# A decoder layer with routed experts: eight expert tiles are run between the last routing steps

## What is computed

```python
logits = xf @ Wg.T
topw, topi = jax.lax.top_k(jax.nn.softmax(logits), 2)
topw = topw / topw.sum(axis=-1, keepdims=True)
for e in range(16):
    h = silu(xf @ W1[e]) * (xf @ W3[e])
    out = out + gates[:, e:e + 1] * (h @ W2[e])
```

## Time and profile before

| what | us |
|---|---|
| median of 3 runs | 822.67 (821.59 to 822.88) |
| the profiled execution | 823.12 |
| its span, first to last instruction | 821.3 |
| PE busy in the span | 798.6 (97%) |
| POOL busy in the span | 396.8 (48%) |
| mean granted clock of PE | 0.993 |

### The profile page before, as it was taken

How to read it: one execution, slowest core, us unless ns; L and a number is a source line. 1 busy time by engine, 2 the same in 40 slices (tenths; PEclk the granted TensorE clock), 3 DMA queues, 4 the chain that set the end, 5 groups by cost and what they waited for, 6 DMA issues and landing times.

```text
span 821.3 us, 21021 instructions
## 1 busy us (share of the span) xinstructions
PE 798.6 (97%) x5949; PEld 758.3 (92%) x5950; DVE 598.0 (73%) x1722; ACT 432.8 (53%) x1185; POOL 396.8 (48%) x567
## 2 busy tenths in 40 slices
PE   9999999999999999999999999999988999999995
PEld 8898999999999999999999999999987799999994
DVE  4757777888787877878787778887675566666663
ACT  4473554637265463737355453726243267667673
POOL 3332134444534454454535444353435358787875
PEclk9999999999999999999999999999999999999997
DMA  8786573655739284564828375573499458777780
GB/s 266 256 290 233 194 256 120 244 204 193 256 125 308 81 281 161 201 242 160 280 95 309 108 254 175 187 263 127 156 425 368 146 106 134 127 132 128 131 132 2
DMA packets 105673, 161.19 MB, mean 196 GB/s; under 512 B 10672, under 2 KB 69616, under 8 KB 104752
## 3 DMA queue, kind: packets, MB, share of 16 engines
q1 hardware_dynamic: 79264, 115.33, 42.0%
q0 software_dynamic: 15792, 35.17, 17.2%
q10 hardware_dynamic: 10576, 10.19, 4.7%
HBM read 50.14 MB, written 112.47 MB: 198 GB/s over the span
## 4 chain that ended last, share of the span: by engine, by line
PE 82%; DVE 6%; ACT 6%; issue 3%; DMA 1%; SPq 1%; POOL 1%; POOLq 0%; DVEq 0%; ACTq 0%
PE ps L797 70%; PE ps L808 5%; PE ps L1037 3%; PE ps L1147 2%; PE ps L1169 2%; ACT fT_hi L1305 2%; ACT relu_v L1306 2%; ACT phi L1292 1%; DVE fT_lo L1508 1%; DVE snmax L1681 1%; DVE smax L1677 1%; DVE pr L1670 1%; DVE xn_attn L1501 0%; ACT pr L1351 0%; DVE stat L1490 0%
## 5 line engine op out<-in xcount | busy, mean ns | idle before, releaser
L788 POOL DMA_INDIRECT out<-narrow,sidx x79 | 122.4, 1549 | 46.1 <-DVE sidx L1886 20.7
L1220 ACT ACTIVATE xn3T<-ps 128x512 f32<-128x512 f32 x17 | 10.2, 597 | 138.8 <-PE ps L808 136.2
L797 PE MATMUL ps<-w_hi,fT_hi 128*128 128x256 f32 x256 | 79.8, 312 | 2.4 <-DVE fT_lo L1508 2.1
L1292 ACT ACTIVATE phi<-ps,nmax 128x128 f32<-128x128 f32 x256 | 73.4, 381 | 9.2 <-DVE nmax L1629 9.0
L1508 DVE TENSOR_TENSOR fT_lo<-relu_v,fT_hi 128x512 fp32r<-128x512 f32 x64 | 52.3, 818 | 33.2 <-ACT relu_v L1306 33.0
L797 PE MATMUL ps<-w_lo,fT_hi 128*128 128x256 f32 x256 | 72.3, 282 | 0.0
L797 PE MATMUL ps<-w_hi,fT_lo 128*128 128x256 f32 x256 | 72.2, 282 | 0.0
L1306 ACT ACTIVATE relu_v<-ps,b_sb 128x256 f32<-128x256 f32 x128 | 69.1, 540 | 0.0
L1305 ACT ACTIVATE fT_hi<-ps,b_sb 128x256 fp32r<-128x256 f32 x128 | 68.0, 531 | 1.5 <-PE ps L797 1.5
L605 POOL TENSOR_TENSOR veps<-mv,eps_ln 128x2 f32<-128x2 f32 x48 | 10.8, 225 | 118.4 <-DVE mv L1494 118.4
L797 PE MATMUL ps<-hT_hi,w_hi 128*128 128x256 f32 x256 | 67.2, 284 | 0.0
(11 more groups left out here) (300 smaller groups left out, 2744.6 us busy)
## 6 DMA issues: line engine op xcount, KB each, us to landing
expert_rows<-zero_rows SPq DMA_DIRECT2D x16, 4352.0 KB, 16.0
narrow<-expert_rows ACTq DMA_DIRECT2D x71, 136.0 KB
expert_up_hi<-X SPq DMA_DIRECT2D x16, 352.0 KB, 2.7
e_lo<-expert_up_lo POOLq DMA_DIRECT2D x2, 2816.0 KB, 12.8
e_hi<-expert_up_hi POOLq DMA_DIRECT2D x2, 2816.0 KB, 22.1
part_raw<-in_E SPq DMA_DIRECT2D x30, 176.0 KB
expert_up_lo<-part_raw SPq DMA_DIRECT2D x15, 352.0 KB, 3.1
X<-in_x SPq DMA_DIRECT2D x16, 256.0 KB
```

Of the source, the lines that this page charges most:

```text
L788: pool.indirect_dma_start(out_rows, bass.IndirectOffsetOnAxis(sidx[:, u:u + 1], 0), yg[:, u, :], None, bounds_check=NT * P - 1, oob_is_err ...
L797: return pe.matmul(out_, lhsT, rhs, start=start, stop=stop)
L1220: return act.activation(out_, in_, ACT.Copy)
L1292: last = act.activation(phi[:, g, h, :], ps[:, g, h * M:(h + 1) * M], ACT.Exp, bias=nmax[:, g, h:h + 1])
```

## The change

Eight slots become early ones. Their plan is made in turns 16 and 17 from the counts of the first 13 sequences (`early_count`, `early_order`, `early_tiles`, `early_taken`, `early_waits` on DVE): experts are ordered by their number of full tiles, and the first eight full tiles in that order are slots 0 to 7. By the counts above these are seven of expert 14 and one of expert 7. SP loads them in turn 17 (`load_early`). Turn 18 goes away: the router of the last sequence, its choice, its counts, its place and its stores are written between slots 0 and 1 of the experts, the plan of the other 71 slots between slots 1 and 3.

The text of the last router on PE now stands ahead of slot 0 (`last_router_rows`, `router(NSEQ - 1, 4)`); ACT copies the rows of the last sequence (`own_rows`) behind the first two roundings; POOL computes the odds with a power (`choice_odds`), which ACT did with an exponential before, and gathers the edges between scatters 1 and 2 (`gather_edges`). The meeting of tiles is worked out in slots 9 to 11, now from both ends of the two tiles, and SP holds slot 8 for it. For the early slots a slot of another expert always counts as meeting, and slots 8 and 9 always wait for slots 6 and 7.

`yg` and `sidx` become rings of 16 (`RING`); `xg` stays at 8. ACT loads tiles 8 to 13 at one place, at the end of slot 6 (`load_late`). The weights are loaded earlier: the low up parts of 14 experts in turn 15, and all up parts by SP. 24 slots are written out, then three rounds of 16, then 7. The matmuls that only kept PE busy behind the last cross attention and ahead of the experts (`keep_clock`: 8, then 9 and 10 calls, and 2 ahead of the last count) go away.

```diff
+    EARLY = 8
+    RING = 2 * GB
+    EARLY_SEQS = NSEQ - 3
+    UNROLLED = 3 * GB
 ...
-            for u in range(GB):
-                step(u, u, False)
-            with eng.Fori(0, (SLOT_TILES // GB - 2) // 2) as g:
+            for s in range(UNROLLED):
+                step(s, s % RING, False)
+            with eng.Fori(0, (SURE - UNROLLED) // RING) as g:
 ...
                 if last_cross:
+                    load_early()
 ...
+            def load_early():
+                sp.wait_ge(early_plan, EARLY_TILES)
+                sp.wait_ge(zeroed, 16 * (NSEQ + 1))
+                sp.wait_ge(placed, EARLY_SEQS * 16 * TOPK * TS)
+                tiles = [tile_of(s) for s in range(3)]
+                sp.wait_ge(snmax_ready, NSEQ)
+                for s in range(GB):
+                    load_tile(s, tiles[s] if s < len(tiles) else tile_of(s))
 ...
-                if isinstance(s, int) and s == 1:
+                if isinstance(s, int) and s == EARLY:
                     sp.wait_ge(ranges_ready, 1)
 ...
+            choice_odds()
+            store_rows(NSEQ - 1)
+            in_groups(slot_tiles, pool)
 ...
-                if last_cross:
-                    keep_clock(2, 7)
-                if b is not None and not last_ffn:
+                if b is not None and not last_ffn and not last_cross:
                     turn_router_rows(b, 7)
 ...
-            keep_clock(2, 10)
+            last_router_rows()
             turn_rows(0, 0)
             turn_rows(1, 1)
+            router(NSEQ - 1, 4)
+            pe.wait_ge(em_loaded, 16 * 6)
             up(0, 0)
 ...
+                if first(s):
+                    count_choices(NSEQ - 1, 5)
+                    pe.wait_ge(logit_ready, NSEQ)
+                if isinstance(s, int) and s == 1:
+                    pe.wait_ge(ps_read, 2)
+                if isinstance(s, int) and s == 3:
+                    pe.wait_ge(plan_ready, 1)
 ...
+            def load_late():
+                act.wait_ge(plan_ready, 1)
+                tiles = [tile_of(s) for s in range(EARLY, EARLY + 2)]
+                act.wait_ge(placed, NSEQ * 16 * TOPK * TS)
+                for s in range(EARLY, 2 * EARLY - 2):
+                    load_rows(s, s, tiles[s - EARLY] if s - EARLY < len(tiles) else tile_of(s))
 ...
+                if isinstance(s, int) and s == EARLY - 2:
+                    load_late()
+                    rows_hi(s + 2, (u + 2) % RING)
 ...
+                if first(s):
+                    place_own(NSEQ - 1, 5)
+                    dve.wait_ge(egap_ready, NSEQ)
+                    gates(NSEQ - 1)
 ...
+                if isinstance(s, int) and s == 1:
+                    late_count()
+                    late_sum()
+                if isinstance(s, int) and s == 2:
+                    late_tiles()
 ...
-                if isinstance(s, int) and s in (1, 2, 3):
-                    (edge_rows, meeting_tiles, numbers_of_tiles)[s - 1]()
+                if isinstance(s, int) and s == EARLY + 1:
+                    edge_rows()
+                if isinstance(s, int) and s == EARLY + 2:
+                    meeting_tiles()
+                if isinstance(s, int) and s == EARLY + 3:
+                    numbers_of_tiles()
```

More of the change, by code:

```diff
@@ L29 @@
+import math
 from contextlib import ExitStack
@@ L597, in _ @@
             pool.wait_ge(const_ready, N_CONST - 2)
-            for whole, short in ((before, before_01), (ones, ones_01)):
-                pool.tensor_copy(short[:, :], whole[:, :]).then_inc(const_ready, 1)
+            for whole, short in ((before, before_01), (ones[:, :], ones_01)):
+                pool.tensor_copy(short[:, :], whole).then_inc(const_ready, 1)
             pool.wait_ge(const_ready, N_CONST)
@@ L720, in turn @@
                         split_ctx(b + 1)
-                if r is not None and not last_turn:
+                if r is not None:
                     keep_rows(r)
@@ L1613, in logits_in, with choice_seen, summed @@
                     .then_inc(logit_ready, 1)
+            def choice_seen(r):
+                hold(dve, chosen, (r + 1) * CHOICE_STEPS)
+                dve.tensor_tensor(oh[:, :, :], hot[:, 0], hot[:, 1], ALU.add).then_inc(oh_ready, 1)
+                if not first(r):
+                    dve.wait_ge(egap_ready, r)
+                dve.tensor_tensor(gap[:, :], best[:, :, 1], best[:, :, 0], ALU.subtract)\
+                    .then_inc(gap_ready, 1)
+            def summed(counted):
+                cum, cbufs, n = counted, (cum_a, cum_b), 1
+                while n < NE:
+                    dst = cbufs[0]
+                    cbufs = cbufs[::-1]
+                    dve.tensor_copy(dst[:, 0:n], cum[:, 0:n])
+                    then(dve.tensor_tensor(dst[:, n:], cum[:, n:], cum[:, 0:NE - n], ALU.add))
+                    cum, n = dst, 2 * n
+                return cum
@@ new lines, in early_waits @@
+            def early_waits():
+                dve.wait_ge(early_plan, EARLY_TILES)
+                for k in range(1, ADDING):
+                    last = dve.tensor_tensor(other_early[:, k - 1, k:], expert_i[:, k:EARLY], expert_i[:, 0:EARLY - k],
+                                             ALU.not_equal)
+                then(last)
+                for k in range(1, ADDING):
+                    last = dve.scalar_tensor_tensor(added_need[:, k - 1, k:EARLY], other_early[:, k - 1, k:], 16.0,
+                                                    round_of[:, 0:EARLY - k], ALU.mult, ALU.add)
+                last.then_inc(early_plan, 1)
```

492 lines of the change are left out of this document (300 added, 192 removed).

## The result

The change makes the kernel slower: 829.83 us median of four runs (828.44 to 831.42) against 822.35 for the kernel before in the same comparison, a ratio of 1.0092 (95% interval 1.0078 to 1.0107). The forecast was 822.9, no change, with 827.5 as the upper end. The profiled execution took 828.44, the fastest of the four; its span is 826.3 and its mean clock 0.985.

The account below looks back on a forecast made before the run. POOL's scatter queue was taken to be as near the bound as PE. The last scatter 2.3 us earlier plus 2.5 for the clock gave +0.2 on 823.12, carried to the median as 822.9, no change; range 818.0 to 827.5.

Parts of the forecast that it names:

- The frame: POOL's scatter queue sets the last scatter's start: first scatter at 644.3, plus 144.3 at 1.85 us each, plus 23.5 of waits.
- the 644 to 647: Sign that the prediction is right: scatter 0 starts near 644 to 647 us; its sum put it at 644.3.
- The waits of slots 7, 8 and 10: On POOL, extra waits of 3.4 for scatter 7, 5.5 for scatter 8 and 3.4 for slot 10.
- the wait of scatter 6: POOL waits 2.2 us for the `yg` of slot 6, ready at 659.3; the scatter starts at 660.2.
- PE turns them by 644.5: The plan's columns are ready at 643.9; PE turns them by 644.5 and only then goes on with slot 3.
- Three slots of 2.0: After turning the plan's columns, PE needs three slots of 2.0 us, to 650.5; ACT ends slot 6 at 652.5.
- 4.4 in all: `load_late` on ACT: six DMA issues of 0.34 plus a hold, and six tile-number reads of 0.32, with nothing covering them.
- hold: Extra time beside the 0.34 us of the DMA issues in `load_late` on ACT; 0.07 was taken.
- Tile 8 to `yg` and the scatter, 3.3: After `load_late`: tile 8's rounding, `up(8)` and silu precede slot 6's `yg`, ready at 659.3; POOL starts 0.9 later.
- The clock: PE falls to 1.2 GHz after idle gaps before 631.2, during the plan and during `load_late`: 2.5 us, between 0 and 5.0.
- one or two falls: Likeliest case: PE's clock falls after one or two of its three gaps, giving 822.0 to 823.7; chance 0.45.
- Rival 1: All three PE gaps bring full or repeated 1.2 GHz spells on the path to slot 8: 825.4 to 827; chance 0.25.

## Why the prediction was wrong

**What held.** The frame: the sum goes by scatters, POOL is the bound to the end, and PE's share is no guide. Scatter 0 at 645.77 lies in the 644 to 647 that were named, partly by luck: the last router's transposes came 0.9 earlier than put (630.32 against 631.2), which hid part of the 2.1 that the clock cost. The waits of slots 7, 8 and 10 came as worked out: 3.2, 5.4 and 3.7 beyond the pace of 1.85, where 3.4, 5.5 and 3.4 were taken. The weights cost nothing: PE has no wait for them, its up matmuls follow the last router's. The ring gains nothing that shows, as said.

**Where it failed: the wait of scatter 6.** It was taken as 2.2 and is 6.4 (666.17 - 657.93 - 1.85). The start of scatter 6 was put at 660.2 and came 6.0 later. By the steps of the prediction:

- "PE turns them by 644.5": 645.75, 1.25 late, since the first spell at 1.2 GHz stood on the path of the last routing. From the transposes to this turn it is 15.4 here and 13.6 with all gaps filled, so the spell cost 1.8, of which the early transposes gave back 0.9.
- "Three slots of 2.0": there are four, slots 3 to 6 (the turn ahead of slot 3 starts at 646.28, `turn_hidden(6)` at 654.02). I had counted one slot too few. ACT ended slot 6 at 654.98, not 652.5: 1.2 more, the slot and 0.5 for the turn itself, less 1.0, since ACT was done 1.0 behind `turn_hidden(6)` where 2.0 had been taken.
- `load_late` "4.4 in all": ACT does nothing else for 6.0 (654.98 to 660.99), 1.6 more. The issue at 0.34 and the read at 0.32 were priced right: they took 0.34 and 0.28, the first of each 0.37 and 0.44. The term that was too small is the "hold": by the chain some 0.35 stands around each issue (the second starts 0.70 behind the first with no read between), where 0.07 had been taken, and the first issue starts 0.65 behind the end of the second read (655.32 to 655.97). So an issue with all that belongs to it takes 0.98, not 0.73.
- Tile 8 to `yg` and the scatter, 3.3: 5.2, of which 1.6 is the half rate (3.19 against 1.57).

1.25 + 1.2 + 1.6 + 1.9 is the 6.0. That leaving slot 6 free takes the wait away, the run with the loads spread shows: 0.91 idle ahead of scatter 6.

**The clock** was a term of 2.5 between bounds of 0 and 5.0. Two of the three gaps were followed by a fall, as "one or two falls" had it; but a spell lasted 6.8 us and not 3.3, so that the first cost 2.1 where at most 1.65 had been allowed. It came to 3 to 5 in all. Rival 1 had this mechanism right and its price too low, and it did not have the loads. What the Trainium skill says there (TensorE: Matmul & The Clock Gate, "Why this matters for your kernels"), that an idle array goes back to half rate, holds for the first and third gap of the changed kernel. The second gap was followed by a fall in seven of the ten executions that left it unfilled, and by none in the three others.

**The rest:** 0.5 more between scatters 8 and 12, and 1.3 more behind scatter 12 (128.78 where 66 times 1.85 plus 5.4 is 127.5). Scatters 13 to 60 start 1.85 to 2.15 apart but for four, 20, 26, 29 and 52, which start 2.8 to 3.1 behind the one before. The "14 such matmuls" and "18" of `keep_clock` are records, two for each matmul; nothing in the sum rests on them.

Together: scatter 8 is 5.65 later than forecast without the clock, 0.5 and 1.3 come behind it, 7.45; 2.5 of it had been charged to the clock, and 4.95 is what the last scatter is late (819.55 against 812.1 + 2.5). The medians differ from the forecast by 6.9 (829.83 less 822.9). Of the 2.0 that remain, 1.8 is that the profiled execution lay 1.4 below its median here and 0.45 above it before.

So the loss was no price of running tiles early. Moved off slot 6, the loads let the change come out even; with the meeting moved and the first gap filled as well it gains 0.4%. Left open: why the clock falls behind the second gap in some executions and not in others, and what a filled second gap would add to the best version (not tried; by its rows at most the 1 us by which scatter 6 is later than back to back).

## What to carry to other kernels

When work is moved forward, the transfers that used to start it one by one start in a bunch; spread their issues over the steps ahead, and look at what stands behind the bunch on the issuing engine's queue, since that queue and the first landing both set the restart. Price a row of instructions on a queue by the distance between the starts of two neighbours, not by adding up what each is shown to take: here some 0.35 us around each issue was in neither. Fill a gap of PE only up to its length, and look at the next gap as well, in more than one execution: behind the same gap the clock fell in some and not in others.

## What the hardware showed that was not expected

- A spell at 1.2 GHz is not of one length: 3.4 us in the kernel before, 6.8 twice in one execution of the changed one, 6.8 and 10.2 in another, 10.2 in the run with the loads spread (629.6 to 639.8). The third gap of the changed kernel and the first of the run with the loads spread had it begin while PE was still idle.
- A gap of the same length, 2.65 us, was followed by no fall in the changed kernel and by 3.4 us at 1.2 GHz in the one with the first gap filled; and with the same text up to there, by a fall with the ring of 8 and by none with that of 16.
- An fp32 matmul of 128 x 256 shows as two records, 0.44 us for the pair in a stream: 18 records in 4.05 us where 9 fillers were written. Counting records as matmuls halves the price.
